# All W2 transfers from tile 2 on issued by ScalarE, two a tile, with SyncE left to W1

## The chip, the cores and the metric

The kernel runs on one core of a Trainium2 chip. The metric is the device time of one execution in microseconds (us), as the median of several runs. Engines are called PE (TensorE), DVE (VectorE), ACT (ScalarE), POOL (GpSimd) and SP (SyncE); "L430" is line 430 of the kernel before.

## The reference

A graph network with 625 nodes of 512 features and 20,000 edges, in two layers, each with a graph part and a feed-forward part, all added to `x`. The last part is what this change touches: 16 experts, each with `W1` (512 x 2048) and `W2` (2048 x 512) in float32, 4 MB each. A router gives each row one leaf (expert):

```python
def body(acc, params):
    w1, bb1, w2, bb2, m = params
    h = jax.nn.gelu(xf @ w1 + bb1, approximate=False)
    y = h @ w2 + bb2
    return (acc + m[:, None] * y, None)
out, _ = jax.lax.scan(body, jnp.zeros_like(xf), (W1, b1, W2, b2, onehot.T))
```

## The kernel before, in words

Up to about 285 us the kernel does the two graph parts and the first feed-forward part, the router, and a table of tiles. The rest, the expert stage, computes only the rows that each expert was given. A tile is one expert with up to 64 rows (one tile, number `LARGE` = 10, takes 32 more). With these inputs there are 16 tiles, 0 to 15, in pairs `p`, with `b` the tile's place in the pair, so tile `i = 2p + b`. Experts beyond the first few are read from a table (`tab`) at run time.

PE does, per tile (`tile`, L1027): the first layer (L1050, halves `h` of the hidden width and `k` blocks of W1), transposes of the hidden rows (L1071), the bias row (L1099), the transposes of the next tile's input rows (`turn_rows`, L995), and the second layer in four quarters q = 0 to 3 (`second_a`, L1118). ACT does the gelus (L691) and copies the result out of PSUM (L703). DVE copies the hidden rows. POOL (`move_rows`, L540) does, in this order for every tile: gather the rows of tile i+2 (L511), wait for ACT's copy of tile i and scatter it with an addition (L519), hold until that scatter has landed, and go to the next tile.

Weights: W1 has two buffers `w1_sb[0..1]` and a third, `w1_two`, put together from tiles that are free by then, used for tiles 2 and 5. W2 has two buffers `w2_sb[0..1]`. Tiles 0 and 1 are loaded far ahead. From tile 2 on, every load waits for its buffer's last user: W1 on `s_w1u` (PE is through the first two blocks) and `s_h` (first layer done), W2 on `s_l2`, which PE raises after each quarter of the second layer. All these loads are issued by SP, in an order written out by hand (L380 to L447): W1 of tile 3 in four blocks, W2 of tile 2 in four pieces of 1 MB (L386 to L390, each behind one quarter of tile 0), then by turns `load_w1(i)` (L404) and `load_w2(i-1)` (L420), and from tile 8 on `load_w1(i)`, `load_w2(i)`. A half of W1 or W2 is one transfer of 2 MB. The last half of the last W2 goes as two of 1 MB, the second on its own semaphore `s_w2_end` (L426 to L428), for which PE waits before the last quarter (L1113). Transfers issued by one engine go through one queue: SP's is called q1 in the profile, POOL's q0.

Of the kernel before, what the change touches and what calls it, by code (L numbers as in the profile page):

```python
# [56 lines left out]
NE, HID = 16, 2048  # L57
# [14 lines left out]
def build(nc, x, src, dst, Wconv, bconv, Wlin, blin, Wa, ba, Ws, bs, Wg, bg, Wr, br, W1, b1, W2, b2, out):  # L72
    ctx = ExitStack()
    with ctx:
        ctx.enter_context(nc.allow_non_contiguous_dma(reason="small bias columns"))

        def sb(name, shape, dt=F32):
            return ctx.enter_context(nc.sbuf_tensor(name, shape, dt))

        def sem(name):  # L80
            return ctx.enter_context(nc.semaphore(name))
# [3 lines left out]
        w2_sb = [sb(f"w2_{b}", [128, MH, DIM]) for b in range(2)]  # L85
# [31 lines left out]
        tab = small[0:1, 684:684 + TAB + 2].bitcast(I32)  # L117
# [52 lines left out]
        def ffn_group(g):  # L170

            layer, h, t = g // (2 * NT), g // NT % 2, g % NT
            return (layer, t) + HALVES[h]
# [58 lines left out]
        s_edges, s_x, s_wconv, s_blin, s_cols = (sem(n) for n in ("edges_in", "x_in", "wconv_in", "blin_in", "cols_in"))  # L232
        s_wlin, s_ffnw, s_win, s_gw, s_bg2 = (sem(n) for n in ("wlin_in", "ffnw_in", "win_in", "gnnw_in", "bg2_in"))
        s_w1 = [[sem(f"w1_in{b}_{j}") for j in range(2)] for b in range(2)]
        s_w1_two, s_w2_end, s_w1q = sem("w1_in_tiles2_5"), sem("w2_in_end"), sem("tile0_w1_block_used")
        s_w2 = [[sem(f"w2_in{b}_{h}") for h in range(2)] for b in range(2)]
        s_iota, s_ident, s_rev, s_ones, s_loops, s_winz = (sem(n) for n in
            ("iota_ready", "ident_ready", "rev_ready", "ones_ready", "loops_ready", "win_cleared"))
# [31 lines left out]
        s_h, s_hc, s_hT, s_gelu, s_l2 = (sem(n) for n in ("hidden_bank", "hidden_copied", "hidden_transposed", "gelu_done", "expert_out"))  # L270
# [17 lines left out]
        def _(sp):  # L288
# [33 lines left out]
            for q, (w, b) in enumerate(((Wa, ba), (Ws, bs))):  # L322
                for s in range(2):
                    for f0, i0 in ((0, 0), (2, 35)):
                        for f in range(2):
                            r = (2 * q + s) * GT + 2 * (f0 + f) + s
# [26 lines left out]
            def w1_block(e, k):  # L353
                j, r = k // 2, k % 2
                return W1[e, j * 256:(j + 1) * 256, :].rearrange("(p r) n -> p r n", r=2)[:, r, :]
# [24 lines left out]
            for k in range(KD):  # L380
# [2 lines left out]
                else:  # L383
                    sp.wait_ge(s_h, 2)
                sp.dma_start(w1_sb[0][:, k, :], w1_block(3, k)).then_inc(s_w1[0][k // 2], 16)
            for q in range(4):  # L386
                h, r = q // 2, q % 2
                sp.wait_ge(s_l2, q + 1)
                sp.dma_start(w2_sb[0][:, 4 * q:4 * q + 4, :],
                             W2[2, h * HID // 2:(h + 1) * HID // 2, :].rearrange("(p m) n -> p m n", p=128)[:, 4 * r:4 * r + 4, :]).then_inc(s_w2[0][h], 16)  # L390
            sp.wait_ge(s_table, 1)
            load_end = sp.value_load(npairs_t[0:1, 1:2], min_val=NE // 2 - 2, max_val=MAX_PAIRS - 2)

            def expert(i):
                return sp.value_load(tab[0:1, bass.ds(i, 1)], min_val=0, max_val=NE - 1)
# [8 lines left out]
            def load_w1(i, b, user):  # L404

                e = expert(i)
                for j in range(2):
                    half_used(j, user)
                    sp.dma_start(w1_sb[b][:, 2 * j:2 * j + 2, :],
                                 W1[bass.ds(e, 1), j * 256:(j + 1) * 256, :].rearrange("a (p r) n -> p (a r) n", r=2)).then_inc(s_w1[b][j], 16)  # L410

            def load_w1_five():

                e = expert(5)
                for k in range(KD):
                    j, r = k // 2, k % 2
                    half_used(j, 2)
                    sp.dma_start(w1_two[k], W1[bass.ds(e, 1), j * 256:(j + 1) * 256, :].rearrange("a (p r) n -> p (a r) n", r=2)[:, r, :]).then_inc(s_w1_two, 16)

            def load_w2(i, b, end=False):  # L420

                e = expert(i)
                for h in range(2):
                    w = W2[bass.ds(e, 1), h * HID // 2:(h + 1) * HID // 2, :].rearrange("a (p m) n -> p (a m) n", p=128)
                    sp.wait_ge(s_l2, 4 * (i - 2) + 2 * h + 2)
                    if end and h == 1:  # L426
                        sp.dma_start(w2_sb[b][:, 8:12, :], w[:, 0:4, :]).then_inc(s_w2[b][1], 16)
                        sp.dma_start(w2_sb[b][:, 12:16, :], w[:, 4:8, :]).then_inc(s_w2_end, 16)  # L428
                    else:
                        sp.dma_start(w2_sb[b][:, 8 * h:8 * h + 8, :], w).then_inc(s_w2[b][h], 16)  # L430

            load_w1(4, 1, user=1)
            load_w2(3, 1)
            load_w1_five()
            load_w2(4, 0)
            load_w1(6, 0, user=3)
            load_w2(5, 1)
            load_w1(7, 1, user=4)
            load_w2(6, 0)
            load_w2(7, 1)  # L440
            with sp.Fori(3, load_end) as p:
                for b in range(2):
                    load_w1(2 * p + b + 2, b, user=2 * p + b)
                    load_w2(2 * p + b + 2, b)
            for b in range(2):
                load_w1(2 * load_end + b + 2, b, user=2 * load_end + b)
                load_w2(2 * load_end + b + 2, b, end=(b == 1))  # L447


        @block.gpsimd  # L450
# [119 lines left out]
        def _(act):  # L570
# [81 lines left out]
            for g in range(1, 4 * NT, 2):  # L652
                layer, t, a, b = ffn_group(g)
# [25 lines left out]
            act.wait_ge(s_table, 1)  # L679
            last = act.value_load(npairs_t[0:1, 0:1], min_val=NE // 2 - 1, max_val=MAX_PAIRS - 1)  # L680

            def tile_out(p, b):

                i = 2 * p + b
                more = isinstance(p, int) and i == LARGE
                act.wait_ge(s_bTc, i + 1)
                for rd in range(2):
                    act.wait_ge(s_hT, 2 * i + rd + 1)
                    for j in range(8):
                        m, c = 8 * rd + j, 2 * (j % 4) + j // 4  # L690
                        g = nc.scalar.activation(hT[:, m, :], P[:, 3 + rd, c * SA:(c + 1) * SA], ACT.Gelu, bias=bT[b][:, m:m + 1])  # L691
                        if j % 4 == 3:
                            g.then_inc(s_gelu, 1)
                if more:
                    act.wait_ge(s_hTB, 1)
                    for m in range(MH):
                        c = 4 * (m % 4) + m // 4
                        g = nc.scalar.activation(hTB[:, m, :], P[:, 0, c * SB_:(c + 1) * SB_], ACT.Gelu, bias=bT[b][:, m:m + 1])
                        if m % 4 == 3:
                            g.then_inc(s_geluB, 1)  # L700
                act.wait_ge(s_yfree, i + 1)
                act.wait_ge(s_l2, 4 * i + 4)
                nc.scalar.activation(y_sb[b], P[:, 7, 0:256], ACT.Copy).then_inc(s_ycp, 1)  # L703
                if more:
                    nc.scalar.activation(y_sbB, P[:, 5, 0:128], ACT.Copy).then_inc(s_ycpB, 1)

            with act.Fori(0, LARGE // 2) as p:
                for b in range(2):
                    tile_out(p, b)
            for b in range(2):  # L710
                tile_out(LARGE // 2, b)
            with act.Fori(LARGE // 2 + 1, last) as p:
                for b in range(2):
                    tile_out(p, b)
            for b in range(2):
                tile_out(last, b)


        @block.tensor
        def _(pe):  # L720
# [306 lines left out]
            def tile(p, b, end=False):  # L1027

                i = 2 * p + b
                more = isinstance(p, int) and i == LARGE  # L1030
                first = isinstance(p, int) and i == 0
# [74 lines left out]

                def second_a(q):
                    if q % 2 == 0:
                        if b or first:
                            pe.wait_ge(s_w2[b][q // 2], 16 * (p + 1))  # L1110
                        else:
                            pe.wait_ge(s_w2[0][q // 2], 16 * (p + 2))
                    elif end and q == 3:  # L1113
                        pe.wait_ge(s_w2_end, 16)
                    pe.wait_ge(s_gelu, 4 * i + q + 1)
                    for m in range(4 * q, 4 * q + 4):
                        for g in range(2):
                            mm = nc.tensor.matmul(P[g * SA:(g + 1) * SA, 7, 0:256], hT[:, m, :], w2_sb[b][:, m, g * 256:(g + 1) * 256],  # L1118
                                                  start=False, stop=(m == MH - 1))
                    if not more:  # L1120
                        mm.then_inc(s_l2, 1)

                def second_b(q):
# [9 lines left out]
                    mm.then_inc(s_l2, 1)  # L1133

                second_a(0)
                if more:
                    pe.wait_ge(s_hBc, 1)
                    turn(0, 2).then_inc(s_hTB, 1)
                    second_a(1)
                    second_a(2)  # L1140
                    second_b(0)
                    second_b(1)
                    second_a(3)
                    second_b(2)
                    second_b(3)
                    return
# [12 lines left out]
            last = pe.value_load(npairs_t[0:1, 0:1], min_val=NE // 2 - 1, max_val=MAX_PAIRS - 1)  # L1159
# [416 lines left out]
```

## Time and profile before

| what | us |
|---|---|
| median of 3 runs | 583.53 (577.77 to 585.37) |
| the profiled execution | 582.65 |
| its span, first to last instruction | 580.9 |
| PE busy | 529.8 |
| ACT busy | 140.6 |
| POOL busy | 64.6 |
| mean granted TensorE clock | 0.975 of full |

The span is what the rows below are measured in, from its start; the execution's own time is 1.75 us longer. Busy time of an engine leaves out register work, waits and the issue of transfers. The DMA share is the mean busy share of the 16 DMA engines. A line of a timeline merges a run of like instructions and gives the idle time before it and what ended it.

### The profile page before, as it was taken

The numbers are of one execution on the slowest core, as the hardware profiler recorded it, in microseconds if no ns is written. First come the engines' busy times: TensorE is split into PE (matmuls) and PEld (weight loads), VectorE is DVE, ScalarE is ACT, GpSimd is POOL, SyncE is SP. The second block draws the span as 40 slices with busy tenths as digits, with TensorE's granted clock in tenths as the row PEclk, the third lists the DMA queues.
The fourth block names the chain that finished last, engine by engine and source line by source line (L and its number), as shares of the span: only waits on it lengthen the run. The fifth ranks groups of instructions, "written<-read, shape, count | busy, mean of one in ns | idle before, by whom it ended". The sixth has DMA issues, their size and how long they took to land.

```text
span 580.9 us, 10020 instructions
## 1 busy us (share of the span) xinstructions
PE 529.8 (91%) x3215; PEld 287.2 (49%) x3215; DVE 191.5 (33%) x572; ACT 140.6 (24%) x496; POOL 64.6 (11%) x94
## 2 busy tenths in 40 slices
PE   1969999889999999999899799999999999988884
PEld 1536667444457466444454345555444365434332
DVE  5898998664410200256741100111111011100110
ACT  1546666011101011003022112222222042202211
POOL 5000000030000000000002222211211212122011
PEclk9979999999999999998799989999999999989998
DMA  6159920001010020118499999999999999999991
GB/s 126 14 177 429 432 120 19 18 1 71 20 72 1 0 72 0 29 63 275 131 391 417 415 422 422 421 422 420 422 428 415 423 425 417 420 420 427 422 386 34
DMA packets 26224, 145.82 MB, mean 251 GB/s; under 512 B 10447, under 2 KB 12697, under 8 KB 16850
## 3 DMA queue, kind: packets, MB, share of 16 engines
q1 hardware_dynamic: 22994, 142.92, 60.7%
q0 software_dynamic: 3200, 2.50, 2.1%
q8 instruction: 20, 0.33, 0.2%
q14 instruction: 10, 0.08, 0.0%
HBM read 142.38 MB, written 4.72 MB: 253 GB/s over the span
## 4 chain that ended last, share of the span: by engine, by line
PE 68%; DMA 15%; DVE 9%; issue 3%; ACT 1%; POOL 1%; DVEq 1%; ACTq 1%; POOLq 0%; SPq 0%
PE P L1050 14%; PE P L1118 13%; DMA w<-in_L_ffn_W 12%; PE P L924 9%; PE P L934 7%; PE P L760 6%; PE P L943 4%; PE P L1071 2%; DMA out<-XT,C 2%; DVE stats L1268 2%; PE P L761 1%; DVE H L1244 1%; DMA XT<-normed_rows,C 1%; PE P L1099 1%; ACT H L606 1%
## 5 line engine op out<-in xcount | busy, mean ns | idle before, releaser
L1118 PE MATMUL P<-w,FB 128*64 128x256 f32 x1024 | 116.8, 384 | 2.2 <-DMA w<-in_L_ffn_W 2.2
L1050 PE MATMUL P<-w,H 128*64 128x512 f32 x448 | 103.6, 612 | 8.0 <-DMA w<-in_L_ffn_W 7.6
L1118 PEld LDWEIGHTS P<-w,FB 128*64 128x64 f32 x1024 | 72.4, 138 | 40.9 <-issue 7.5
L1526 DVE COPY H<-P 128x512 f32<-128x512 f32 x32 | 22.1, 691 | 212.7 <-PE P L1050 212.6
L691 ACT ACTIVATE FB<-P,FB 128x64 f32<-128x64 f32 x256 | 54.2, 360 | 147.6 <-PE P L1071 147.6
L1050 PEld LDWEIGHTS P<-w,H 128*64 128x64 f32 x448 | 32.6, 142 | 70.6 <-issue 62.5
L760 PE MATMUL P<-H 125*126 125x500 bf16 x176 | 59.3, 415 | 8.1 <-DVE H L1244 4.7
L1244 DVE TENSOR_SCALAR H<-iota,small 125x626 bf16<-125x626 f16 x176 | 56.6, 381 | 8.9 <-issue 6.9
L606 ACT ACTIVATE H<-G,small 125x126 bf16<-125x126 f16 x132 | 44.2, 391 | 36.0 <-PE P L761 22.0
L924 PE MATMUL P<-G,XT 128*125 128x512 f32 x120 | 52.0, 592 | 0.0
L934 PE MATMUL P<-C,H 125*128 125x313 f32 (+1 forms) x160 | 42.4, 425 | 0.0
L760 PEld LDWEIGHTS P<-H 125*126 125x126 bf16 x176 | 25.3, 144 | 32.9 <-ACT H L606 19.6
L761 PE MATMUL P<-H 125*126 125x127 bf16 x176 | 40.2, 228 | 0.0
L1365 DVE TENSOR_SCALAR H<-P,dis_c 125x512 f32<-125x512 f32 x15 | 11.3, 751 | 83.8 <-PE P L924 83.8
L934 PEld LDWEIGHTS P<-C,H 125*128 125x128 f32 x160 | 30.2, 189 | 12.5 <-issue 1.0
L924 PEld LDWEIGHTS P<-G,XT 128*125 128x125 f32 x120 | 22.4, 188 | 27.8 <-issue 27.5
L519 POOL DMA_INDIRECT out<-XT,C x16 | 25.6, 1599 | 75.2 <-ACT XT L703 54.2
L703 ACT ACTIVATE XT<-P 128x256 f32<-128x256 f32 x16 | 6.1, 383 | 89.9 <-PE P L1118 83.3
L761 PEld LDWEIGHTS P<-H 125*126 125x126 bf16 x176 | 25.6, 145 | 0.0
L667 ACT ACTIVATE XT<-P,bg_c 128x313 f32<-128x313 f32 (+1 forms) x16 | 8.3, 522 | 67.9 <-PE P L934 67.9
L505 POOL COPY C<-C 128x1 int32 (+2 forms) x32 | 6.7, 209 | 150.1 <-DMA out<-XT,C 113.1
L1071 PEld LDWEIGHTS P<-ident,H 128*128 128x128 f32 x132 | 14.7, 141 | 14.1 <-issue 12.6
(313 smaller groups left out, 437.1 us busy)
## 6 DMA issues: line engine op xcount, KB each, us to landing
w<-in_L_ffn_W SPq DMA_DIRECT2D x55, 2048.0 KB, 25.8
w<-in_L_ffn_W SPq DMA_DIRECT2D x10, 1024.0 KB, 8.4
G<-in_L_gnn_W SPq DMA_DIRECT2D x3, 1024.0 KB, 5.3
G<-in_L_ffn_W SPq DMA_DIRECT2D x2, 1024.0 KB
C<-in_L_ffn_W SPq DMA_DIRECT2D x2, 1024.0 KB
xs<-in_L_ffn_W SPq DMA_DIRECT2D x2, 1024.0 KB
xn<-in_L_ffn_W SPq DMA_DIRECT2D x2, 1024.0 KB
xs<-in_x SPq DMA_DIRECT2D x1, 1120.0 KB
```

Of the source, the lines that this page charges most:

```text
L519: nc.gpsimd.indirect_dma_start(out=out.rearrange("t (g n) -> (t g) n", g=2), out_offset=bass.IndirectOffsetOnAxis(ap=row_out[b], axis=0), ...
L606: nc.scalar.activation(D[0:NC, j, :], step_at[0:NC, t, :], ACT.Sign, bias=ef[0:NC, 1, j, bass.ds(lo_g + u, 1)], scale=-1.0).then_inc(s_dho ...
L691: g = nc.scalar.activation(hT[:, m, :], P[:, 3 + rd, c * SA:(c + 1) * SA], ACT.Gelu, bias=bT[b][:, m:m + 1])
L760: nc.tensor.matmul(P[0:DW, b0, 0:GROUP], D[0:NC, j, :], S[0:NC, j, 0:GROUP], start=False, stop=False, skip_group_check=True)
L761: nc.tensor.matmul(P[0:DW, b0 + 1, 0:LAST], D[0:NC, j, :], S[0:NC, j, GROUP:GROUP + LAST], start=False, stop=False, skip_group_check=True) ...
L924: mm = nc.tensor.matmul(P[0:NC, c, :], XTn[:, k, c * NC:(c + 1) * NC], Gw[:, k, :], start=(k == 0), stop=(k == KD - 1))
L934: mm = nc.tensor.matmul(P[:, (5 + g) % 8, 0:b - a], Hn[0:NC, c, m * 128:(m + 1) * 128], C[0:NC, c, a:b], start=(c == 0), stop=(c == NCH - 1))
L943: mm = nc.tensor.matmul(P[0:NC, (5 + t) % 8, :], C[0:NC, c, t * NC:(t + 1) * NC], Hn[0:NC, c, :], start=(c == 0), stop=(c == NCH - 1))
L1050: mm = nc.tensor.matmul(P[g * SA:(g + 1) * SA, h, :], xT[b][:, k, :], w1a[k][:, h, g], start=(k == 0), stop=(k == KD - 1))
L1071: t = nc.tensor.transpose(P[:, to, j * 128:(j + 1) * 128], h_sb[:, h, j * 128:(j + 1) * 128], ident[:, :])
L1118: mm = nc.tensor.matmul(P[g * SA:(g + 1) * SA, 7, 0:256], hT[:, m, :], w2_sb[b][:, m, g * 256:(g + 1) * 256], start=False, stop=(m == MH - 1))
L1244: hot = ts(S[0:NC, j, 0:NPAD], iota[0:NC, :], ef[0:NC, 0, j, bass.ds(lo_g + u, 1)], None, ALU.is_equal)
```

## The change

SP no longer loads any W2 after tile 1. ACT gets a `load_w2` of its own, called twice a tile in `tile_out`, after the gelus of tile i and before the copy of its result: it reads the expert of tile i+2, waits for quarter 2 (then quarter 4) of tile i's second layer, and issues one half of W2, 2 MB. This holds from tile 2 on, so that tile 2's W2 comes in two pieces and the last W2 in two as well; `s_w2_end` is gone. SP's queue holds W1 alone, in the same order. PE's waits for W2 are counted anew.

```diff
@@ -232,7 +232,7 @@
         s_edges, s_x, s_wconv, s_blin, s_cols = (sem(n) for n in ("edges_in", "x_in", "wconv_in", "blin_in", "cols_in"))
         s_wlin, s_ffnw, s_win, s_gw, s_bg2 = (sem(n) for n in ("wlin_in", "ffnw_in", "win_in", "gnnw_in", "bg2_in"))
         s_w1 = [[sem(f"w1_in{b}_{j}") for j in range(2)] for b in range(2)]
-        s_w1_two, s_w2_end, s_w1q = sem("w1_in_tiles2_5"), sem("w2_in_end"), sem("tile0_w1_block_used")
+        s_w1_two, s_w1q = sem("w1_in_tiles2_5"), sem("tile0_w1_block_used")
         s_w2 = [[sem(f"w2_in{b}_{h}") for h in range(2)] for b in range(2)]
         s_iota, s_ident, s_rev, s_ones, s_loops, s_winz = (sem(n) for n in
             ("iota_ready", "ident_ready", "rev_ready", "ones_ready", "loops_ready", "win_cleared"))
@@ -383,11 +383,6 @@
                 else:
                     sp.wait_ge(s_h, 2)
                 sp.dma_start(w1_sb[0][:, k, :], w1_block(3, k)).then_inc(s_w1[0][k // 2], 16)
-            for q in range(4):
-                h, r = q // 2, q % 2
-                sp.wait_ge(s_l2, q + 1)
-                sp.dma_start(w2_sb[0][:, 4 * q:4 * q + 4, :],
-                             W2[2, h * HID // 2:(h + 1) * HID // 2, :].rearrange("(p m) n -> p m n", p=128)[:, 4 * r:4 * r + 4, :]).then_inc(s_w2[0][h], 16)
             sp.wait_ge(s_table, 1)
             load_end = sp.value_load(npairs_t[0:1, 1:2], min_val=NE // 2 - 2, max_val=MAX_PAIRS - 2)
 
@@ -417,34 +412,15 @@
                     half_used(j, 2)
                     sp.dma_start(w1_two[k], W1[bass.ds(e, 1), j * 256:(j + 1) * 256, :].rearrange("a (p r) n -> p (a r) n", r=2)[:, r, :]).then_inc(s_w1_two, 16)
 
-            def load_w2(i, b, end=False):
-
-                e = expert(i)
-                for h in range(2):
-                    w = W2[bass.ds(e, 1), h * HID // 2:(h + 1) * HID // 2, :].rearrange("a (p m) n -> p (a m) n", p=128)
-                    sp.wait_ge(s_l2, 4 * (i - 2) + 2 * h + 2)
-                    if end and h == 1:
-                        sp.dma_start(w2_sb[b][:, 8:12, :], w[:, 0:4, :]).then_inc(s_w2[b][1], 16)
-                        sp.dma_start(w2_sb[b][:, 12:16, :], w[:, 4:8, :]).then_inc(s_w2_end, 16)
-                    else:
-                        sp.dma_start(w2_sb[b][:, 8 * h:8 * h + 8, :], w).then_inc(s_w2[b][h], 16)
-
             load_w1(4, 1, user=1)
-            load_w2(3, 1)
             load_w1_five()
-            load_w2(4, 0)
             load_w1(6, 0, user=3)
-            load_w2(5, 1)
             load_w1(7, 1, user=4)
-            load_w2(6, 0)
-            load_w2(7, 1)
             with sp.Fori(3, load_end) as p:
                 for b in range(2):
                     load_w1(2 * p + b + 2, b, user=2 * p + b)
-                    load_w2(2 * p + b + 2, b)
             for b in range(2):
                 load_w1(2 * load_end + b + 2, b, user=2 * load_end + b)
-                load_w2(2 * load_end + b + 2, b, end=(b == 1))
 
 
         @block.gpsimd
@@ -679,7 +655,14 @@
             act.wait_ge(s_table, 1)
             last = act.value_load(npairs_t[0:1, 0:1], min_val=NE // 2 - 1, max_val=MAX_PAIRS - 1)
 
-            def tile_out(p, b):
+            def load_w2(i, b, h):
+
+                e = act.value_load(tab[0:1, bass.ds(i + 2, 1)], min_val=0, max_val=NE - 1)
+                act.wait_ge(s_l2, 4 * i + 2 * h + 2)
+                act.dma_start(w2_sb[b][:, 8 * h:8 * h + 8, :],
+                              W2[bass.ds(e, 1), h * HID // 2:(h + 1) * HID // 2, :].rearrange("a (p m) n -> p (a m) n", p=128)).then_inc(s_w2[b][h], 16)
+
+            def tile_out(p, b, end=False):
 
                 i = 2 * p + b
                 more = isinstance(p, int) and i == LARGE
@@ -698,6 +681,9 @@
                         g = nc.scalar.activation(hTB[:, m, :], P[:, 0, c * SB_:(c + 1) * SB_], ACT.Gelu, bias=bT[b][:, m:m + 1])
                         if m % 4 == 3:
                             g.then_inc(s_geluB, 1)
+                if not end:
+                    load_w2(i, b, 0)
+                    load_w2(i, b, 1)
                 act.wait_ge(s_yfree, i + 1)
                 act.wait_ge(s_l2, 4 * i + 4)
                 nc.scalar.activation(y_sb[b], P[:, 7, 0:256], ACT.Copy).then_inc(s_ycp, 1)
@@ -713,7 +699,7 @@
                 for b in range(2):
                     tile_out(p, b)
             for b in range(2):
-                tile_out(last, b)
+                tile_out(last, b, end=True)
 
 
         @block.tensor
@@ -1106,12 +1092,7 @@
 
                 def second_a(q):
                     if q % 2 == 0:
-                        if b or first:
-                            pe.wait_ge(s_w2[b][q // 2], 16 * (p + 1))
-                        else:
-                            pe.wait_ge(s_w2[0][q // 2], 16 * (p + 2))
-                    elif end and q == 3:
-                        pe.wait_ge(s_w2_end, 16)
+                        pe.wait_ge(s_w2[b][q // 2], 16 * (p + 1))
                     pe.wait_ge(s_gelu, 4 * i + q + 1)
                     for m in range(4 * q, 4 * q + 4):
                         for g in range(2):
```

## Rows read from the trace of the kernel before

**Rows 1.** The page: busy us (share) and instructions; POOL's queue (packets, MB, share).

```profile
PE 529.8 (91%) x3215; PEld 287.2 (49%) x3215; DVE 191.5 (33%) x572; ACT 140.6 (24%) x496; POOL 64.6 (11%) x94
...
q0 software_dynamic: 3200, 2.50, 2.1%
```

**Rows 2.** Windows: PE, PEld, DVE, ACT, POOL busy (x); PEclk, DMA share, GB/s.

```profile
295.00:300.00 5.00, 5.00 (x67) 3.65 (x68) 2.65 (x10) 3.06 (x15) 0.00 (x0) 1.00 0.95 354
...
400.00:450.00 50.00, 50.00 (x354) 25.75 (x352) 5.67 (x12) 12.76 (x59) 9.17 (x12) 1.00 1.02 423
568.00:570.00 2.00, 2.00 (x22) 1.34 (x20) 0.00 (x0) 0.23 (x2) 0.00 (x0) 1.00 0.19 82
```

**Rows 3.** PE's timeline (start, us, line, idle before) at the end; one wait.

```profile
515.00 8.78 PE L1050 MATMUL P<-w,H 128*64 128x512 f32 x32 [2.59 <-DMA w<-in_L_ffn_W]
...
535.50 3.65 PE L1050 MATMUL P<-w,H 128*64 128x512 f32 x16 [1.37 <-DMA w<-in_L_ffn_W]
...
555.77 3.65 PE L1050 MATMUL P<-w,H 128*64 128x512 f32 x16 [1.23 <-DMA w<-in_L_ffn_W]
560.57 3.65 PE L1050 MATMUL P<-w,H 128*64 128x512 f32 x16 [1.15 <-DMA w<-in_L_ffn_W]
...
565.91 7.13 PE L1118 MATMUL P<-w,FB 128*64 128x256 f32 x64
...
PE P L1050 <- DMA w<-in_L_ffn_W: 7.6, 5, 2.6
```

**Rows 4.** PE's timeline, tiles 2 to 4.

```profile
333.06 0.51 PE L995 MATMUL P<-ident,XT 128*128 128x128 f32 x2 [3.71 <-DMA XT<-normed_rows,C]
...
342.52 7.03 PE L1050 MATMUL P<-w,H 128*64 128x512 f32 x32
...
358.49 7.04 PE L1050 MATMUL P<-w,H 128*64 128x512 f32 x32
...
366.62 0.51 PE L995 MATMUL P<-ident,XT 128*128 128x128 f32 x2
```

**Rows 5.** POOL's timeline: gathers (L511) and scatters (L519).

```profile
326.01 1.07 POOL L511 DMA_INDIRECT XT<-normed_rows,C  x1 [0.89 <-POOL C L505]
...
328.31 1.61 POOL L519 DMA_INDIRECT out<-XT,C  x1 [1.00 <-POOL C L505]
...
344.13 1.61 POOL L519 DMA_INDIRECT out<-XT,C  x1 [4.09 <-issue]
...
356.36 1.08 POOL L511 DMA_INDIRECT XT<-normed_rows,C  x1 [0.86 <-POOL C L505]
```

**Rows 6.** SP's timeline of issues, early and late.

```profile
297.73 7.99 SPq L389 DMA_DIRECT2D w<-in_L_ffn_W  x4
...
520.26 4.03 SPq L409 DMA_DIRECT2D w<-in_L_ffn_W  x2
...
534.30 0.33 SPq L427 DMA_DIRECT2D w<-in_L_ffn_W  x1
```

**Rows 7.** Gathers: first (L526), then 8 from 350 us on (L511).

```profile
L526 POOL DMA_INDIRECT XT<-normed_rows,C x1: 1252/1252/1252, 286.5 to 286.5; - x1
...
DMA to landing us min/median/max: 3.0/3.0/3.0
...
L511 POOL DMA_INDIRECT XT<-normed_rows,C x8: 1072/1072/1082, 356.4 to 469.2; - x8
...
DMA to landing us min/median/max: 6.5/7.0/7.7
```

**Rows 8.** Scatters (L519): the last one, then all 16.

```profile
L519 POOL DMA_INDIRECT out<-XT,C x1: 1566/1566/1566, 574.3 to 574.3; - x1
...
DMA to landing us min/median/max: 3.3/3.3/3.3
...
L519 POOL DMA_INDIRECT out<-XT,C x16: 1566/1602/1642, 312.9 to 574.3; - x16
...
DMA to landing us min/median/max: 3.3/10.6/11.5
```

## Prediction

> **What bounds the kernel now.** I read the page's busy shares first, then the windows over the expert stage, then TensorE's and SyncE's timelines at its end, then GpSimd's. PE is busy 91% of the span and ACT 24% [rows 1], so PE looks like the bound. In the windows the reader is to see a second one: from 295 us on the DMA share is 0.95 or more, in the window 400 to 450 it is 1.02 at 423 GB/s, and it falls only at the very end, to 0.19 at 568 to 570 [rows 2]. PE in turn has no gap there either (50.00 of 50 us busy).
>
> Which of the two sets the end is told by PE's timeline. Where it has its weights, a tile takes 358.49 - 342.52 = 15.97 us [rows 4]. At the end it goes slower: the first layer of tile 14 starts at 535.50, that of tile 15 at 555.77, 20.27 us later, with a wait for W in front of each half, and the second half of tile 15's W1 comes at 560.57 [rows 3]. So the 8 MB of weights of a tile cost 20.3 us of transfers against 16.0 us of PE. PE lives on what was loaded ahead until about 512 us, and after that it follows the transfers. All PE waits for weights in front of L1050 together are 7.6 us in 5 times [rows 3]: the two bounds are nearly level, and the transfers have nothing to spare. After the last matmul (565.91 + 7.13 = 573.04) come a copy and a scatter, 7.9 us to the end of the span.
>
> A third chain runs beside these and is easily missed, since GpSimd is hardly busy. GpSimd gathers the rows of tile i+2, scatters the result of tile i, holds until the scatter has landed, and goes on. Its timeline [rows 5]: gather at 326.01, scatter at 328.31 (2.3 us later, with the result long there), scatter at 344.13 and the next gather at 356.36 (12.2 us later: landing, hold and pick). So one round of this loop can't be shorter than 2.3 + 12.2 = 14.5 us, just under PE's 16.0. The gather of 356.36 lands some 7.0 us after its start [rows 7], at 363.4, and PE wants it at 366.62 [rows 4]: 3.2 us to spare. At 333.06 there was nothing to spare, and PE waited 3.71 us for a gather [rows 4].
>
> **The change part by part.**
>
> *W2 leaves SP's queue.* The order of issue hardly changes. SP issued each piece as its buffer came free, and in time a tile's W1 buffers come free before its W2 buffers and those before the next tile's W1. The issue pair at 520.26 and the single one at 534.30 follow PE's progress [rows 6]; no W1 was held up behind a W2 that wasn't yet allowed. So there is no head-of-line wait to gain back, and I cost this at 0. The bytes are the same too.
>
> *ACT issues two transfers a tile.* An issue takes 0.33 us on SP [rows 6]; with the register loads I take 0.45 us for one on ACT, not shown here, between 0.3 and 1.5. The first of a tile goes out after ACT's gelus, while ACT waits for PE anyway. The second stands between the last matmul of the second layer and the copy L703 of the result: the result reaches GpSimd 0.45 us later. Queued behind the new waits are only that copy and the next tile's gelus, which need PE's next first layer, 7 us on. Alone this costs nothing; in the GpSimd chain it adds 0.45 us (bounds 0.3 to 1.5).
>
> *Tile 2's W2 comes in two pieces of 2 MB and not in four of 1 MB.* The first piece went out at 297.73 [rows 6], after one quarter of tile 0's second layer; now it waits for two quarters, some 1.8 us. The share in the window 295 to 300 is 0.95 [rows 2], so the queue is nearly dry just there. Every microsecond of idle transfer is paid at the end as long as transfers bound it: 1.8 us, bounds 0 and 3.
>
> *The last 2 MB comes whole.* Transfers run at 20.27 / 4 = 5.07 us for 2 MB. From 560.5, when the last W1 has landed, W2's first half lands at 565.6, the third quarter at 568.1 and the last at 570.7 (by this rate). PE's third quarter needs 568.1 now and would need 570.7; without that it would start at 565.9 + 3.6 = 569.5. So 1.2 us, bounds 0 and 2.5.
>
> *Two queues of weights instead of one.* This is the term that decides. Row by row: a scatter lands 3.3 us after its start when no weights are moving (the last one), and in 10.6 us in the median beside the one weight queue [rows 8]; a gather 3.0 us alone and 7.0 us beside it [rows 7]. The weight queue thus costs a scatter 7.3 us and a gather 4.0 us, though it takes no part in their bytes: a mean of 2.50 MB / 33 = 76 KB each [rows 1], 0.2 us at 423 GB/s; their small packets stand behind large ones. With two weight queues that both hold work, a small packet stands behind one of each. Price of that: 7.3 and 4.0 us more, if they take turns one for one; 0 if the engines share by time of arrival. The trace of before has no second queue of this kind, so bounds are 0 and 7.3 (scatter), 0 and 4.0 (gather). I take the upper ends, since the one queue's effect is so far above what the bytes explain.
>
> The Trainium skill ("DMA: Bandwidth & Descriptors", Queues, rings and completion order) states that each DMA engine goes round robin between the queue rows that hold work, a packet at a time, and that SP and ACT own one row each. By it a gather's or scatter's packets would wait for two weight packets in place of one, as reckoned above; the trace so far shows only the step from none to one.
>
> Followed through on one gather: the scatter of 344.13 would land 7.3 us later, the gather of 356.36 start at 363.7 and land in 11.0 us at 374.7, and PE wants it at 366.62. That is 8 us late. PE waits there before its second layer, where before it waited for nothing. The loop's floor becomes 14.5 + 7.3 = 21.8 us a tile, above the 20.3 us of the transfers. It can't stay there: if the loop is the slowest, transfers finish early, one queue runs empty for part of the time and the scatter gets faster again. So I take 20.3 us a tile for the loaded stretch, and PE's 16.0 us for tiles 3 to 5, where few transfers are outstanding.
>
> *The sum.* Before, tile 2 ended at 342.52, the start of tile 3's first layer [rows 4]. After: 3 us later (the gather that PE waited for at 333.06 gets later; bounds 0 and 11), 345.5. Tiles 3 to 13: 3 x 16.0 + 8 x 20.3 = 210.4, so 555.9. Tiles 14 and 15: 2 x 16.0 on weights that have by now come ahead of PE, plus one gather wait of 4: 591.9. Then 7.9 to the end of the span and 1.75 from span (580.9) to the execution's own time (582.65): 601.5. The median of the runs, 583.53, is 0.9 above the profiled execution. Forecast: 602 us. Note what gives: before, PE spent the PE-bound pace early and waited late, and had tile 13 done at 534, when SP issues for it [rows 6]; now it loses its lead in gather waits, and finishes well behind the transfers. The 1.8 and 1.2 us of the two edits on W2 are hidden behind this.
>
> **The rivals.**
>
> *The scatters don't get slower, and nothing much happens.* If the engines serve the small packets as before however many weight queues there are, the loop stays at 14.5 us, and only 1.8 + 1.2 us are left: 586.5 us, within 2%. For it: the loaded landing may be waiting in a common store rather than turns. Against: nothing beyond that. It decides as long as a scatter lands in under 12 us (14.5 + 1.5 = PE's 16.0). Not slower, in what can be measured.
>
> *The loop stays fully loaded.* If both queues hold work nearly all the time, 11 tiles at 21.8 us are 240 and the head is late by up to 11: 342.5 + 11 + 240 + 36 + 9.7 = 639 at worst. Half of what that lies above 602, so 620 us, is what I price. Against it is the balance above: 21.8 us a tile is more than the weights need.
>
> *Two queues move more.* The rate in the middle is 423 GB/s at a share of 1.02 [rows 2]; if the second queue closed gaps between packets worth 4% and the scatters stayed fast, the 280 us of loading (about 288 to 568) would shrink by 11: 572 us. Against it, the share leaves no gap to close. The Trainium skill says as much ("DMA: Bandwidth & Descriptors", Rules for kernel authors): spreading DMAs over issuing engines doesn't help bandwidth, as they use the same 16 DMA engines.
>
> **How the numbers follow.** The chain through GpSimd at 592 to 612: 0.60. Scatters as before, 586.5: 0.23. Fully loaded, about 620: 0.13. More bandwidth, 572: 0.04. The likeliest gives 602. The range reaches down to the second case (586) and up to near the third (619). What a measurement of this kernel can tell from no change is about 2%, 572 to 595: faster 0.03, same 0.26, slower 0.71.
>
> **What would show it.** Right: scatters (L519) landing in 15 to 18 us and gathers in 9 to 11; PE's L995 waiting for a DMA on normed rows in most tiles from 4 on, several us each; almost no wait of L1050 or L1118 for weights at the end; DMA share under 1 over the last 20 us of PE's work; a tile period near 20 us already at 400 us. Wrong: scatters still at 10 to 12 us with PE unbroken to 500 us. The forecast then falls to the second case. If the period is above 21 us at 400 us, the third holds.

## The result, and the profile after

The changed kernel takes 599.53 us in the median, 581.77 before in the same runs: ratio 1.0307, 95% interval 1.0229 to 1.0386, so slower. The profiled execution took 600.7 us, with a span of 598.9. In a later set of runs the changed kernel gave 600.48 (ratio 1.0351, interval 1.0301 to 1.040). In the experiments below e5, e7, e9 and e10 each have one run at a lower granted clock among theirs (in e10 one of 908 us), and leaving these out moves no median by more than 0.9 us.

The page after: busy shares, and the queues (packets, MB, share of the 16 engines). It answers to [rows 1].

```profile
PE 533.2 (89%) x3215; PEld 290.2 (48%) x3215; DVE 191.9 (32%) x572; ACT 141.4 (24%) x497; POOL 64.5 (11%) x94
...
q1 hardware_dynamic: 18530, 84.19, 35.8%
q10 hardware_dynamic: 4032, 58.72, 23.4%
q0 software_dynamic: 3200, 2.50, 2.1%
```

The reader is to see that the same engines are as busy as before (PE 3.4 us more), and that ACT's queue, q10, now carries 58.72 MB, 28 halves of W2. Nothing in the shares says why 18 us are gone. The waits do (engine and line, what for: us in total, times, longest us), from 285 us on:

```profile
POOL C L481 <- DMA out<-XT,C: 189.6, 14, 17.3
...
PE P L981 <- DMA XT<-normed_rows,C: 27.4, 8, 6.5
```

L981 is the transpose of the next tile's input rows (L995 before). PE waits 27.4 us in 8 times for gathers, where before it was once, 3.7 us [rows 4]. It waits for no weights at all; before, those waits were 9.8 us (7.6 of them in [rows 3]). The sum: 27.4 - 3.7 - 9.8 = 13.9 us of waits, with 3.4 us of longer matmuls 17.3 of the 18.0 us by which the span grew.

The chain of work that ended last, over the whole span, says the same (by line; before, then after): the scatters' landings have grown from 2% of the span to 26%, and the weights, 12% before, are gone from it.

```profile
PE P L1050 14%; PE P L1118 13%; DMA w<-in_L_ffn_W 12%; PE P L924 9%; PE P L934 7%; PE P L760 6%; PE P L943 4%; PE P L1071 2%; DMA out<-XT,C 2%; DVE stats L1268 2%; PE P L761 1%; DVE H L1244 1%; DMA XT<-normed_rows,C 1%; PE P L1099 1%; ACT H L606 1%
...
DMA out<-XT,C 26%; PE P L910 9%; PE P L920 7%; PE P L1099 7%; PE P L746 6%; PE P L1036 4%; DMA XT<-normed_rows,C 4%; PE P L929 4%; DVE stats L1249 2%; POOL XT L487 1%; DVE H L1225 1%; PE P L747 1%; PE P L1057 1%; PE P L825 1%; PE P L770 1%
```

What stands behind it is GpSimd's timeline (start, us; L487 gathers, L495 scatters), beside [rows 5], and the landings, beside [rows 7] and [rows 8]:

```profile
358.06 1.08 POOL L487 DMA_INDIRECT XT<-normed_rows,C  x1 [0.86 <-POOL C L481]
...
360.35 1.60 POOL L495 DMA_INDIRECT out<-XT,C  x1 [1.00 <-POOL C L481]
...
378.62 1.08 POOL L487 DMA_INDIRECT XT<-normed_rows,C  x1 [0.87 <-POOL C L481]
...
381.00 1.60 POOL L495 DMA_INDIRECT out<-XT,C  x1 [1.10 <-issue]
```

```profile
L495 POOL DMA_INDIRECT out<-XT,C x16: 1566/1602/1642, 311.9 to 592.1; - x16
...
DMA to landing us min/median/max: 3.1/15.4/18.3
...
L487 POOL DMA_INDIRECT XT<-normed_rows,C x14: 1042/1073/1107, 304.1 to 557.9; - x14
...
DMA to landing us min/median/max: 7.1/7.9/11.6
```

Before, a scatter landed in 10.6 us in the median and a gather in 7.0; now in 15.4 and 7.9 (the worst gather 11.6). One round of the loop, 358.06 to 378.62, is 20.6 us. The scatter is issued 2.3 us behind the gather with an idle of only 1.00 us that is GpSimd's own: the result had long been there, so the loop waits for itself. Its shortest, by these medians, is 2.3 + 1.5 (from the landing to the next gather) + 15.4 = 19.2 us; from the gather of 338.27 to that of 557.88 its 11 rounds took 20.0 us each in the mean.

PE's timeline after (start, us, idle before it in brackets), beside [rows 3] and [rows 4]:

```profile
338.87 7.04 PE L1036 MATMUL P<-w,H 128*64 128x512 f32 x32
...
354.84 7.04 PE L1036 MATMUL P<-w,H 128*64 128x512 f32 x32
...
366.61 0.51 PE L981 MATMUL P<-ident,XT 128*128 128x128 f32 x2 [3.56 <-DMA XT<-normed_rows,C]
...
552.76 7.04 PE L1036 MATMUL P<-w,H 128*64 128x512 f32 x32
...
565.75 0.70 PE L981 MATMUL P<-ident,XT 128*128 128x128 f32 x2 [4.78 <-DMA XT<-normed_rows,C]
...
574.99 7.03 PE L1036 MATMUL P<-w,H 128*64 128x512 f32 x32
...
583.71 7.13 PE L1099 MATMUL P<-w,FB 128*64 128x256 f32 x64
```

The gather of 358.06 is wanted at 363.05 and lands at 366.61: 3.56 us of wait. Tile 3 still takes 15.97 us; from tile 4 on the mean is near 20 (tiles 3 to 13: (552.76 - 338.87) / 11 = 19.4 us; before, (535.50 - 342.52) / 11 = 17.5 us). Both means hold tile 10, the large one, which takes 25.0 us in either kernel. At the end PE works on alone. The windows (PE, PEld, DVE, ACT, POOL busy; PEclk, DMA share, GB/s) beside [rows 2]:

```profile
400.00:450.00 50.00, 43.33 (x280) 21.99 (x278) 5.67 (x12) 11.13 (x50) 6.76 (x9) 0.93 1.01 424
560.00:570.00 10.00, 5.22 (x32) 3.20 (x32) 0.97 (x2) 3.49 (x16) 1.59 (x1) 0.83 0.82 329
570.00:580.00 10.00, 10.00 (x72) 4.91 (x70) 0.00 (x0) 0.38 (x1) 1.95 (x3) 1.00 0.05 7
```

The weights are all in at about 570 us, as before, but PE ends at 590.84 and not at 573.04. Transfers lost little; PE lost its place behind them.

### The profile page after: what moved, and what is told of

The parts are those of the page before. It is cut to its first block, busy times and chain, and to the rows that moved or that the text cites. A ratio compares the mean times of both kernels' runs of the same rounds, so it can differ in the third digit from the quotient of the medians.

```text
span 598.9 us, 10083 instructions
## 1 busy us (share of the span) xinstructions
PE 533.2 (89%) x3215; PEld 290.2 (48%) x3215; DVE 191.9 (32%) x572; ACT 141.4 (24%) x497; POOL 64.5 (11%) x94
## 3 DMA queue, kind: packets, MB, share of 16 engines
q10 hardware_dynamic: 4032, 58.72, 23.4%
## 4 chain that ended last, share of the span: by engine, by line
PE 47%; DMA 30%; DVE 9%; issue 7%; POOL 3%; ACT 1%; DVEq 1%; POOLq 1%; ACTq 1%; SPq 0%
DMA out<-XT,C 26%; PE P L910 9%; PE P L920 7%; PE P L1099 7%; PE P L746 6%; PE P L1036 4%; DMA XT<-normed_rows,C 4%; PE P L929 4%; DVE stats L1249 2%; POOL XT L487 1%; DVE H L1225 1%; PE P L747 1%; PE P L1057 1%; PE P L825 1%; PE P L770 1%
## 5 line engine op out<-in xcount | busy, mean ns | idle before, releaser
L1099 PE MATMUL P<-w,FB 128*64 128x256 f32 x1024 | 123.5, 401 | 0.0
L1036 PE MATMUL P<-w,H 128*64 128x512 f32 x448 | 100.6, 600 | 0.4 <-issue 0.4
L1099 PEld LDWEIGHTS P<-w,FB 128*64 128x64 f32 x1024 | 75.5, 145 | 42.8 <-issue 10.7
L920 PEld LDWEIGHTS P<-C,H 125*128 125x128 f32 x160 | 30.2, 189 | 12.5 <-issue 1.0
L981 PE MATMUL P<-ident,XT 128*128 128x128 f32 x32 | 8.9, 364 | 29.5 <-DMA XT<-normed_rows,C 27.4
L495 POOL DMA_INDIRECT out<-XT,C x16 | 25.6, 1599 | 40.5 <-ACT XT L689 19.0
## 6 DMA issues: line engine op xcount, KB each, us to landing
w<-in_L_ffn_W SPq DMA_DIRECT2D x30, 2048.0 KB, 19.1
xs<-in_L_ffn_W SPq DMA_DIRECT2D x2, 1024.0 KB, 10.9
```

The lines of the kernel that those rows point to most:

```text
L495: nc.gpsimd.indirect_dma_start(out=out.rearrange("t (g n) -> (t g) n", g=2), out_offset=bass.IndirectOffsetOnAxis(ap=row_out[b], axis=0), ...
L920: mm = nc.tensor.matmul(P[:, (5 + g) % 8, 0:b - a], Hn[0:NC, c, m * 128:(m + 1) * 128], C[0:NC, c, a:b], start=(c == 0), stop=(c == NCH - 1))
L1036: mm = nc.tensor.matmul(P[g * SA:(g + 1) * SA, h, :], xT[b][:, k, :], w1a[k][:, h, g], start=(k == 0), stop=(k == KD - 1))
```

## The experiments

"Theory" is that a second weight queue slows the scatters and so lengthens GpSimd's loop beyond the tile's time.

**e1: the two size edits alone, all on SP's queue.** Left out of the change: ACT's queue.

```diff
-            for q in range(4):
...
+            for h in range(2):
+                sp.wait_ge(s_l2, 2 * h + 2)
...
-                    if end and h == 1:
-                        sp.dma_start(w2_sb[b][:, 8:12, :], w[:, 0:4, :]).then_inc(s_w2[b][1], 16)
-                        sp.dma_start(w2_sb[b][:, 12:16, :], w[:, 4:8, :]).then_inc(s_w2_end, 16)
+                    sp.dma_start(w2_sb[b][:, 8 * h:8 * h + 8, :], w).then_inc(s_w2[b][h], 16)
```

> The kernel before with only the two size edits: W2 of tile 2 in two pieces of 2 MB behind quarters 2 and 4, and the last half of the last W2 whole; all still on SP's queue. Theory (the second weight queue slows GpSimd's scatters): the sizes cost 0 to 3 us, so 582 to 587 us, and scatters stay at 10 to 11 us. Rival (the sizes are the cause): near 599 us.

Measured: 584.64 us, ratio 1.0076 (1.0034 to 1.0118), 4.2 us over the 580.44 of before (4.4 by the ratio); scatters 10.7 us. So the sizes cost some 4 us where weights set the end; the last wait shows how (PE's timeline at the end of e1):

```profile
561.58 3.65 PE L1045 MATMUL P<-w,H 128*64 128x512 f32 x16 [1.14 <-DMA w<-in_L_ffn_W]
...
571.69 3.67 PE L1108 MATMUL P<-w,FB 128*64 128x256 f32 x32 [1.09 <-DMA w<-in_L_ffn_W]
```

PE waits once more, in front of the last two quarters, for the whole 2 MB. In the changed kernel PE waits for no weights, so nothing in its trace puts these 4 us into its 18.

**e2: the changed kernel with a late hold.** GpSimd holds for scatter i-1 after it has issued scatter i. (The first and the last tiles are written out apart from the loop for this; not shown.)

```diff
-                hold(s_yst[b], 16 * p + 16)
+                if b:
+                    hold(s_yst[0], 16 * p + 16)
+                else:
+                    hold(s_yst[1], 16 * p)
                 pool.sem_inc(s_yfree, 1)
...
```

> The changed kernel, but GpSimd holds for the scatter of tile i-1 behind the issue of the scatter of tile i, so that a scatter's landing no longer stands in front of the next gather. Theory: scatters still land in 15 us or so, but the gathers start some 10 us earlier, PE waits for no gather, and the time is again set by the weights: 582 to 588 us. Rival (two queues bring the weights in worse, or in a worse order): still 595 to 600 us, with PE waiting for W.

Measured: 586.37 us (ratio 1.0131, 1.0059 to 1.0204). Scatters still land late, 15.8 us in the median; 10 to 12 of the 18 us are back (5.9 us over before are left, 7.6 by the ratio). The weights are on two queues as before this edit, so most of the cost is the place of the scatter in GpSimd's loop, not the loading. Two gather waits of PE, 9.4 us in all, are left against what was expected, beside 7.4 us in 3 times for W2. Nearly all of the 9.4 is one:

```profile
516.93 0.70 PE L990 MATMUL P<-ident,XT 128*128 128x128 f32 x2 [8.05 <-DMA XT<-normed_rows,C]
```

This gather was issued at 494.60 behind both scatters of the large tile (486.67 and 488.58), for which GpSimd had not yet held; they landed in 17.1 and 25.1 us and the gather in 22.3. How the rest of the loss divides between this wait, the waits for W2 and the sizes of e1 is not shown.

**e3: the same late hold in the kernel before.** The same edit, with one weight queue.

> The same late hold in the kernel before. Theory: the loop was just under the tile period there and the weights set the end, so nothing but the one early gather wait goes: 579 to 584 us. Rival (the hold costs time in any kernel): 570 us or less.

Measured: 581.54 us, ratio 1.0017 (0.9976 to 1.0058). No change: PE reaches its first wait for weights sooner and waits longer for them, 15.3 us in all and not 9.8. The hold is free as long as the loop is under the tile's time.

**e4: the changed kernel with 8 KB rows.** A row is here the piece that lies together for one partition: 16 KB in a transfer of 2 MB. All halves of W1 and W2 as two transfers each, but for W2 of tiles 0 and 1 (the counts that PE waits for are changed to suit, not shown):

```diff
-                    sp.dma_start(w1_sb[b][:, 2 * j:2 * j + 2, :], ...
+                    for r in range(2):
+                        sp.dma_start(w1_sb[b][:, 2 * j + r, :], ...
...
-                act.dma_start(w2_sb[b][:, 8 * h:8 * h + 8, :], ...
+                for r in range(2):
+                    act.dma_start(w2_sb[b][:, 8 * h + 4 * r:8 * h + 4 * r + 4, :], ...
```

> The changed kernel with every 2 MB weight transfer made as two of 1 MB, whose rows are 8 KB in place of 16 KB on each partition; bytes, queues and waits for buffers are as in the changed kernel. Theory (small packets take turns with large ones, one from each queue): a turn is half as long, so scatters land in 9 to 11 us and the time falls to 582 to 590 us. Rival (the scatters are slowed by the load as such, not by turns): scatters stay at 15 us and the time at 597 to 602 us.

Measured: 593.66 us (ratio 1.023, 1.0151 to 1.0308). The landings did as expected, the time did not. The landings, and the two largest waits of PE in e4:

```profile
DMA to landing us min/median/max: 3.3/10.8/12.3
...
PE P L1102 <- DMA w<-in_L_ffn_W: 15.5, 5, 4.5
...
PE P L984 <- DMA XT<-normed_rows,C: 3.7, 1, 3.7
```

Scatters land in 10.8 us beside two weight queues, not 15.4: as expected if what they stand behind is half as long. The gather waits are gone but for one. In their place PE waits 15.5 us for W2 (L1102 is the second layer), each time in front of its second half: W1 of the next tile comes in beside W2 of this one. That is a second cost of two queues, not in the prediction; e5 and e8 say what it is worth.

**e5: 8 KB rows in the kernel before.**

> The kernel before with every 2 MB weight transfer made as two of 1 MB with 8 KB rows, all on SP's queue: the other half of e4. Theory (turns between one weight queue and POOL's, each as long as one row): scatters land in 6.5 to 8.5 us, not 10.6, and the time stays at 578 to 584 us, as the weights set it and are in order. Rival (1 MB transfers are dearer in themselves, which would explain that e4 stayed at 594): 588 us or more.

Measured: 584.98 us (ratio 1.006, 1.0018 to 1.0102), just over the range expected; scatters 8.4 us, also nearer the upper end. So 1 MB transfers cost 3.5 us in themselves by the ratio (4.9 by the medians), and can't explain the 13 us of e4. Nor can the sum of the waits: with one queue PE waits 16.4 us for weights, no less than the 15.5 of e4. The order does. The last wait for weights ends at nearly the same time in both, 562.59 here and 563.24 in e4, but it is for W1's second half of tile 15 here, 12.5 us from PE's end, and for W2's second half of tile 14 in e4, 21.0 us from it. Side by side, the scatter's median landing:

| | 16 KB rows | 8 KB rows |
|---|---|---|
| no weights moving | 3.3 | 3.3 |
| one weight queue | 10.6 | 8.4 |
| two weight queues | 15.4 | 10.8 |

**e6: only the first halves of W2 on ACT's queue.** e1, with the `h = 0` transfers issued by ACT; 29.36 MB on q10.

> e1, with only the first half of each W2 issued by ACT; the second halves stay on SP's queue in their old place. A quarter of the bytes is on the second queue, so it holds work for about half of the time. Theory: scatters between those of e1 (10.7) and of the changed kernel (15.4), 12 to 14 us in the median; few gather waits of PE; 585 to 592 us. Rival (any use of the second queue costs the whole): 597 us or more.

Measured: 593.47 us (ratio 1.0201, 1.0132 to 1.0269), 1.5 us above what was expected; scatters 12.9 us, in between as expected. Part of the bytes on the second queue gives part of the loss: 13 us over before, where e1, with the same sizes and no second queue, has 4. PE's waits are 12.2 us for gathers and 9.6 us for weights, and the latter are for W1's second halves: here W2's first half takes turns with W1.

**e7: ACT's copy of the result in front of its second issue.**

```diff
                     load_w2(i, b, 0)
-                    load_w2(i, b, 1)
                 act.wait_ge(s_yfree, i + 1)
                 act.wait_ge(s_l2, 4 * i + 4)
                 nc.scalar.activation(y_sb[b], P[:, 7, 0:256], ACT.Copy).then_inc(s_ycp, 1)
...
+                if not end:
+                    load_w2(i, b, 1)
```

> The changed kernel with ACT's copy of the result in front of its second W2 issue and not behind it. Theory: the result reaches GpSimd 0.4 us earlier, but GpSimd is behind it in most tiles, so 597 to 600 us. Rival (ACT's issue in the path of the result is what costs): 590 us or less.

Measured: 601.91 us (ratio 1.0354, 1.0287 to 1.0422), no better than the changed kernel (599.53 and 600.48). ACT's issue, 0.34 us in the trace, costs nothing that the time shows.

**e8: both cures, 8 KB rows and the late hold, on two queues.**

> The changed kernel with both cures, 8 KB rows (e4) and the late hold (e2): no wait for gathers is left. Theory of a second cost, the order of the weights (with two queues by turns W1 of the next tile comes in beside W2 of this one, and ahead of its second half): PE still waits 10 us or more for second halves of W2 at L1118's like and ends 13 us or more after the last weights have landed; 587 to 594 us. Rival (the rest of e4's loss came through gathers too): 580 to 585 us.

Measured: 592.69 us (ratio 1.0215, 1.0162 to 1.0267). PE's waits in e8, and its timeline at the last wait:

```profile
PE P L1111 <- DMA w<-in_L_ffn_W: 19.9, 7, 5.0
...
PE P L993 <- DMA XT<-normed_rows,C: 0.9, 1, 0.9
...
540.74 5.36 PE L1111 MATMUL P<-w,FB 128*64 128x256 f32 x32 [3.57 <-DMA w<-in_L_ffn_W]
...
561.16 5.36 PE L1111 MATMUL P<-w,FB 128*64 128x256 f32 x32 [2.54 <-DMA w<-in_L_ffn_W]
...
575.07 7.13 PE L1111 MATMUL P<-w,FB 128*64 128x256 f32 x64
```

Gathers cost 0.9 us and the time is still 12 us over before. Some of that is the 1 MB transfers: over e5, which has them on one queue, it is 7.7 us, and the size edits of e1 may have a part in it. PE waits 19.9 us in 7 times, every time for a second half of W2. The last such wait ends at 561.16, and 5 us of tile 14 and all 16 of tile 15 are still to do then, though tile 15's own weights make PE wait no more. In e5, one queue, the last wait ends at 562.59 in front of W1's second half of tile 15, 12.5 us from PE's end. The bytes come at the same rate and in a worse order. (PE ended 11 us after the last weights, not 13.) The waits are also longer ones: most of e5's are under 1.5 us. Behind them PE is slower in e8, 5.36 us for half a second layer and not 3.67. The windows behind the wait of 3.57 us in e8 and behind one of 1.27 us in e5 (the last three numbers are the granted clock, the DMA share and GB/s):

```profile
540.80:544.00 3.20, 3.20 (x18) 1.94 (x20) 0.00 (x0) 0.00 (x0) 0.00 (x0) 0.54 1.03 430
...
532.10:535.70 3.60, 3.60 (x32) 2.25 (x32) 0.00 (x0) 0.00 (x0) 0.00 (x0) 1.00 1.00 418
```

So of the 7.5 us between the spans of e8 and e5, PE's waits hold 2.4 (20.8 against 18.4 us) and its longer busy time 4.2 (531.7 against 527.5).

**e9: the kernel before with a longer loop and no second queue.** Three operations on a tile that nobody reads any more are added to each round.

```diff
                 hold(s_yst[b], 16 * p + 16)
+                for k in range(3):
+                    nc.gpsimd.tensor_tensor(wmid[:, :, :], wmid[:, :, :], wmid[:, :, :], ALU.subtract).then_inc(s_slow, 1)
+                    hold(s_slow, 3 * i + k + 1)
```

> The kernel before, one weight queue, with three GpSimd operations of some 1.4 us each (5 us in all with their waits) behind every hold for a scatter, so that the loop is as long as in the changed kernel, 14.5 + 4.8 = 19.3 us, with no second queue. Theory (the longer loop is what costs): gathers come late, PE waits for them in half of the tiles, 594 to 602 us. Rival (the second queue costs in some other way): within 1% of before, 578 to 586 us.

Measured: 602.23 us (ratio 1.044, 1.0365 to 1.0515), level with the changed kernel in the same runs (600.48). GpSimd's timeline and PE's waits in e9:

```profile
361.55 1.10 POOL L511 DMA_INDIRECT XT<-normed_rows,C  x1 [0.86 <-POOL C L505]
...
363.85 1.61 POOL L519 DMA_INDIRECT out<-XT,C  x1 [1.00 <-POOL C L505]
374.95 1.25 POOL L553 TENSOR_TENSOR wmid<-wmid 128x640 f32<-128x640 f32 x1 [9.49 <-DMA out<-XT,C]
376.38 1.25 POOL L553 TENSOR_TENSOR wmid<-wmid 128x640 f32<-128x640 f32 x1 [0.18 <-POOL wmid L553]
377.81 1.25 POOL L553 TENSOR_TENSOR wmid<-wmid 128x640 f32<-128x640 f32 x1 [0.18 <-POOL wmid L553]
...
380.92 1.09 POOL L511 DMA_INDIRECT XT<-normed_rows,C  x1 [0.87 <-POOL C L505]
...
PE P L998 <- DMA XT<-normed_rows,C: 28.7, 11, 7.3
```

One weight queue, scatters at 11.0 us, and 4.3 us of added work (three times 1.43): the round is 19.4 us, PE waits 28.7 us for gathers, and the whole loss is there. This is the changed kernel's profile without the change.

**e10: late hold, two queues, and 8 KB rows for W1 only.**

> As e8 (late hold, two queues), but only W1 goes in rows of 8 KB, in transfers of 1 MB; W2 keeps its rows of 16 KB. If the engines take turns by packet, W2's queue gets two thirds of the rate while both hold work. Theory of the order as second cost: W2's second halves are no longer late, PE's waits for them fall from 20 us to under 6, and the time from 592.7 to 584 to 589 us; scatters land in between, 12 to 15 us. Rival (turns are by bytes, or the order doesn't matter): as e8, 591 to 594 us.

Measured: 599.0 us (ratio 1.0351, 1.0301 to 1.040). PE's waits in e10 (L1047 is the first layer), the issues of weights (count, KB each, median us from issue to landing), and the two queues in the window 430 to 440 us (packets, MB, share):

```profile
PE P L1047 <- DMA w<-in_L_ffn_W: 19.5, 5, 7.0
...
PE P L992 <- DMA XT<-normed_rows,C: 2.1, 1, 2.1
...
w<-in_L_ffn_W SPq DMA_DIRECT2D x56, 1024.0 KB, 25.1
w<-in_L_ffn_W ACTq DMA_DIRECT2D x28, 2048.0 KB, 12.9
...
q10 hardware_dynamic: 186, 2.79, 65.5%
q1 hardware_dynamic: 184, 1.34, 32.2%
```

The waits for W2 are gone, as expected of turns by packet. The two queues show the turns themselves: as many packets from each, and twice the bytes from the one with the longer rows. In the changed kernel, with 16 KB rows on both, the window 350 to 360 has 145 packets from each, 2.12 and 2.11 MB. The rival of turns by bytes is out. The time went the wrong way: W1 is now short, and PE waits 19.5 us for it, nearly all in front of second halves; W2's transfers land in 12.9 us in the median and W1's in 25.1, where e8 has 24.4 and 17.1. So the order of the weights matters, and either of the two can be the late one. My expectation took for granted that W1 could spare what W2 got.

**e11: the changed kernel once more.**

> The changed kernel as it stands, beside e9 and e10 on the same chip: 598 to 602 us, scatters 15 us in the median. It is there so that e9 and e10 are compared with it in the same stretch of runs.

Measured: 600.48 us; scatters 14.2 us, gathers 7.8, PE's waits for gathers 30.3 us in 10 times.

Of the versions with a second weight queue e2 came nearest, 1.3% over the kernel before, and none with one queue beat it.

## Why the prediction was right, and which terms were not

- *What bounds.* Two level bounds, weights and PE, and a GpSimd loop 1.5 us under the tile's time: right. e3 shows that the loop costs nothing while it stays under; e9 shows that 4.3 us more in it cost as much as the change did.
- *No head-of-line wait to gain back on SP, at 0.* Nothing was gained, as said. But the single queue had a worth that this step didn't see: its order of issue is the order of need. e8 against e5 shows 7.7 us at most for the loss of that order where gathers are no longer late. In the changed kernel itself it is hidden, since PE is behind the weights anyway. In e2 it isn't seen apart: after the gather wait of 8.05 us at 516.93 PE is behind the weights there too and waits for none, while in e8 the same gather lands in 10.9 us and holds up nothing. What the order costs with 16 KB rows alone stays open.
- *ACT's issues, 0.45 us in the chain.* 0.34 us each in the trace for the issue alone, and e7 shows no cost. Right.
- *The size edits, 1.8 and 1.2 us.* e1 has 4.4 us for both, of which the interval leaves 2 to 7, so the 3.0 predicted is not excluded. Hidden in the changed kernel, as said: no wait for weights is left there.
- *Two queues instead of one, 7.3 and 4.0 us more.* The mechanism was right; the size was off. Measured 4.8 us for a scatter and 0.9 us for a gather in the medians. The prediction laid the whole of the one queue's effect to turns. Half rows take off 2.2 us with one queue (10.6 to 8.4) and 4.6 us with two (15.4 to 10.8). If the part that goes with the row's length is twice what half rows take off, it is 4.4 us with one queue and 9.2 us with two: that part doubles, and the remaining 6.2 us in either case (10.6 - 4.4, 15.4 - 9.2) does not. This split is an estimate from the table under e5, not measured by itself. With the 14.2 us of e11 in place of 15.4 the part with two queues is 6.8 us and the rest 7.4, so that the part grows is shown, and that it doubles is not. The Trainium skill ("DMA: Bandwidth & Descriptors", Queues, rings and completion order) has the turns at packet granularity between rows that hold work; the equal counts of packets in e10 and in the changed kernel (184 and 186, 145 and 145) agree with it.
- *The loop's floor, 21.8 us, held down to the 20.3 us of the weights.* The floor was 19.2 us by the medians and the rounds took 20.0 in the mean. As foreseen, one queue ran empty for part of the time and the rounds were shorter there: from 390 to 400 SP's queue moved 0.02 MB and ACT's 3.13, and the rounds from 378.62 and 396.77 took 18.2 and 17.5 us. That this balance gave the 20.0, and not the size of the landings alone, is not shown. PE's pace was not an even one: it had tiles of 16 us between tiles of 20 to 25, and the 25.0 us of tile 10, PE's own work, were not in the sum. Tiles 3 to 13 took 19.4 us each against 210.4 / 11 = 19.1.
- *Tiles 3 to 5 at 16 us.* Only tile 3 did. Tile 4 took 376.12 - 354.84 = 21.3 us by its neighbours' starts.
- *The start, 3 us later.* It came 3.7 us earlier: 338.87 for tile 3's first layer, 342.52 before, 345.5 predicted. The stage began 2.9 us earlier in this execution (302.27 for tile 1's first layer, 305.18 before), and the gather wait of 3.71 us in front of tile 2's second layer shrank to 0.44, with one of 2.69 us in tile 1: the two scatters up to there landed in 10.4 and 10.2 us, much as before (11.5 and 8.6).
- *The sum.* That it ends 1.1 us off is luck: the start was 6.6 us early, tiles 3 to 13 took 213.9 us and not 210.4, tiles 14 and 15 took 590.84 - 552.76 = 38.1 and not 36. These cancel to 590.84 for PE's end, 591.9 predicted.
- *The rival without slower scatters, 586.5.* It fell by the landings; e1, which is that case, gave 584.64, so its time was rightly priced.
- *The rival of the fully loaded loop, about 620.* It fell: the rounds took 20.0 us in the mean and not 21.8.
- *The rival with more bandwidth.* 422 to 424 GB/s in the middle, as before; it fell.

## What to carry to other kernels

Before moving transfers to another queue, look for small transfers that share the DMA engines and for the chain that waits on their landing; a nearly idle engine with a hold in its loop can be the closest of all bounds, and its slack (1.5 us here) is all that an added queue may cost it. Here, with the weights already at full rate, one queue in order of need was worth more than two: the second added no rate, delayed the small transfers and gave up the order. If the second queue is wanted, take the landing out of the loop first (the late hold of e2 gave back 10 to 12 us), and look again at the gathers, which then stand behind scatters still under way.

## What the runs showed that I had not expected

A wait of PE costs more than its length. The timeline and the windows of the changed kernel around the longest such wait before 450 us:

```profile
443.43 0.70 PE L981 MATMUL P<-ident,XT 128*128 128x128 f32 x2 [5.29 <-DMA XT<-normed_rows,C]
...
444.91 9.33 PE L1099 MATMUL P<-w,FB 128*64 128x256 f32 x64
```

```profile
440.00:442.00 2.00, 0.00 (x0) 0.00 (x0) 0.00 (x0) 0.00 (x0) 0.00 (x0) 1.00 1.05 440
443.50:448.00 4.50, 4.50 (x22) 2.85 (x24) 0.42 (x1) 1.74 (x8) 0.00 (x0) 0.50 1.03 424
450.00:454.00 4.00, 4.00 (x40) 2.64 (x38) 0.00 (x0) 0.00 (x0) 0.15 (x1) 1.00 0.99 422
```

PE had waited 5.29 us, and the second layer behind it took 9.33 us instead of 7.13. The granted clock was still 1.00 at 440 to 442, with PE idle, then 0.50 (the level of 1.2 GHz) at 443.5 to 448, with PE at work again, and 1.00 (2.4 GHz) from 450 on. So it fell after PE had stopped, and rose again only well into the next work. This wait cost 5.3 + 2.2 us; over the whole kernel PE's busy time grew by 3.4 us. Between e4 and e5 it is more: PE is busy for 535.3 us against 527.5 in e5, with 19.2 and 18.4 us of waits. The shortest wait there with a slow stretch behind it is one of 2.26 us, in front of 542.61 (granted clock 0.50 from 544 to 546). The length of the wait alone doesn't tell: behind one of 3.08 us in e6, in front of 530.56, half a first layer took its usual 3.65 us.

The other surprise is e10 against e8: rows of half the length on one of two queues moved 20 us of PE's waits from W2 to W1.
